# Overlapping two batches of sparse attention beside a shared MLP: adjacency written over the sigmoids, halves across batch ends, tallies on ScalarE, additions on GpSimd

## The reference

```python
# adjacency from ctx (4, 512, 128), mixed into the normalized rows of x, per batch
sim = einsum('bhnd,bhmd->bnm', Q, K) / (sqrt(32) * 4)
threshold = top_k(sim, 153)[0][:, :, -1:]          # the 153rd largest of each row
A = sigmoid(sim) * (sim >= threshold)
A = (A + swapaxes(A, -1, -2)) * 0.5
x = x + tanh(g_xattn[0]) * ((1 - gamma) * layernorm(x) + gamma * A)
# then a mixture of experts with a shared MLP over all rows
shared = silu(xn @ sw1) * (xn @ sw3) @ sw2         # xn = layernorm(x), 704 hidden
```

## Time and profile before

| | us |
|---|---|
| median of three runs | 1753.17 (1752.91 to 1756.59) |
| the profiled execution's own time | 1756.12 |
| its span | 1754.3 |
| stage a, from the span's start to the last `y_in` | 399.9 |
| busy in the span: TensorE, VectorE, ScalarE, GpSimd | 1491.5, 1257.5, 749.7, 458.2 |
| first products of batches 0, 1, 2, 3 start at | 98.15, 181.69, 267.63, 345.61 |

### The profile page before, as it was taken

The page is one execution under the profiler, slowest core; times in us unless marked ns, Lnnn a source line. Parts: engine busy times, 40 slices in busy tenths (PEclk is TensorE's granted clock), DMA queues, the critical chain, the costliest instruction groups (busy, mean ns, idle before and its releaser), DMA issues.

```text
span 1754.3 us, 24078 instructions
## 1 busy us (share of the span) xinstructions
PE 1491.5 (85%) x8146; PEld 713.8 (41%) x8146; DVE 1257.5 (72%) x2199; ACT 749.7 (43%) x1312; POOL 458.2 (26%) x436
## 2 busy tenths in 40 slices
PE   2178687891899999379989999998899999999998
PEld 1145344451555656113223233223444544544544
DVE  6987868736788987699988887864665565555555
ACT  5263535222455554247767776773212212222221
POOL 4212121100566665611000000000232323323222
PEclk7589898996999999679999999999999999999999
DMA  5211212113465554554200202127000000000000
GB/s 172 74 44 45 74 36 84 52 37 111 143 189 183 182 180 145 149 121 97 52 10 17 46 0 49 31 30 139 1 1 0 24 0 0 24 0 0 24 12 12
DMA packets 114805, 113.74 MB, mean 65 GB/s; under 512 B 59416, under 2 KB 87320, under 8 KB 114720
## 3 DMA queue, kind: packets, MB, share of 16 engines
q1 hardware_dynamic: 108752, 93.83, 19.8%
q0 software_dynamic: 5680, 18.62, 3.8%
q10 hardware_dynamic: 288, 0.20, 0.1%
HBM read 59.26 MB, written 31.20 MB: 52 GB/s over the span
## 4 chain that ended last, share of the span: by engine, by line
PE 65%; DVE 20%; issue 5%; ACT 4%; POOL 3%; DMA 2%; SPq 1%; DVEq 0%; ACTq 0%; POOLq 0%
PE PS L1982 18%; PE PS L829 12%; PE PS L2005 9%; PE PS L844 6%; PE PS L1445 5%; DVE WORK L1573 4%; PE PS L1434 4%; PE PS L1425 4%; PE PS L1995 2%; ACT BIG L1343 1%; PE PS L837 1%; PE PS L819 1%; DVE WORK L559 1%; DVE WORK L581 1%; PE PS L417 1%
## 5 line engine op out<-in xcount | busy, mean ns | idle before, releaser
L1982 PE MATMUL PS<-BIG 128*128 128x512 f16 x1536 | 342.6, 384 | 9.2 <-DVE BIG L2060 4.6
L1573 DVE TENSOR_REDUCE WORK<-PS 128x2 f32<-128x1024 f32 x256 | 304.0, 1217 | 46.6 <-PE PS L1425 46.1
L1343 ACT ACTIVATE BIG<-PS 128x512 f32<-128x512 f32 x512 | 278.5, 599 | 102.2 <-PE PS L1434 102.0
L1982 PEld LDWEIGHTS PS<-BIG 128*128 128x128 f16 x1536 | 151.5, 99 | 191.7 <-issue 10.8
L1425 PE MATMUL PS<-BIG 128*128 128x512 f16 x512 | 199.1, 396 | 28.2 <-DVE WORK L1573 19.9
L1434 PE MATMUL PS<-BIG 128*128 128x512 f16 x512 | 195.1, 384 | 7.4 <-ACT BIG L1343 3.0
L829 PE MATMUL PS<-BIG,WORK 128*128 (+1 forms) x1128 | 178.8, 316 | 15.3 <-DVE WORK L864 12.8
L2005 PE MATMUL PS<-BIG 128*128 128x512 f16 x768 | 173.8, 379 | 1.8 <-DVE BIG L2080 1.8
L1918 ACT ACTIVATE WORK<-PS 128x512 f32<-128x512 f32 x64 | 38.2, 597 | 307.5 <-PE PS L1982 307.5
L2060 DVE SCALAR_TENSOR_TENSOR BIG<-PS,WORK 128x512 f32<-128x512 f32 x64 | 44.1, 690 | 141.3 <-ACT WORK L1918 141.2
L829 PEld LDWEIGHTS PS<-BIG,WORK 128*128 128x128 f16 x1128 | 108.9, 98 | 77.0 <-issue 20.1
(11 more groups left out here) (244 smaller groups left out, 2204.4 us busy)
## 6 DMA issues: line engine op xcount, KB each, us to landing
wdq_scratch<-WORK SPq DMA_DIRECT2D x48, 256.0 KB
WORK<-in_L_ffn_w_dram SPq DMA_DIRECT2D x32, 352.0 KB, 3.6
y_scratch<-WORK SPq DMA_DIRECT2D x39, 256.0 KB
BIG<-BIG SPq DMA_DIRECT2D x96, 64.0 KB, 2.3
X<-in_x_dram SPq DMA_DIRECT2D x4, 1024.0 KB, 9.0
WORK<-in_L_ffn_w_dram SPq DMA_DIRECT2D x16, 256.0 KB, 2.8
WORK<-in_L_ffn_gate_w_dram SPq DMA_DIRECT2D x16, 256.0 KB, 3.2
WORK<-in_L_ffn_up_w_dram SPq DMA_DIRECT2D x16, 256.0 KB, 3.2
```

The costliest lines, as they stand in the source:

```text
L1343: nc.scalar.activation(PB[:, tp, 2 * h + j, :], BBANK[j], ACT.Exp, scale=SOFT_SCALE).then_inc(exp_ok, 1)
L1573: v.tensor_reduce(MXU[:, g % 2, c:c + 2], APAIR[h % 2], AX_X, ALU.max, negate=True).then_inc(max_ok, 1)
L1982: ins = nc.tensor.matmul(bank[b], fxT[:, p, a, k * P:(k + 1) * P], w[:, c, l, k, :], start=(i == 0), stop=(i == 3 * KD - 1))
```

## The change

- q and k of batches 1 to 3 lie in used parts of `ctxT`. `adjacency` writes over `sig`, not over `sim`, so the next batch's similarities can be copied into `sim` before this batch is mixed. From batch 1 on, similarities go through bank 0, one at a time.
- The halves of all batches form one sequence: `finish(u - 2)` runs across batch ends, banks alternate (`pair_of`), and the turn of half u-1 comes behind the product of half u, except at i = 6 and 7. The next batch's projection stands at i = 5, its similarities at i = 5, 6, 7, its `search_start` and first try at the end.
- Counts: ScalarE applies Sign to th_try - sim and sums (`counts`), for two of four rows in batch 0 and all rows after it. VectorE's step works with S minus twice the count.
- For batches 1 to 3 ScalarE makes tanh of half the value, GpSimd turns it into the gated half sigmoid (`gains`) and adds the masked rows to X (`own_similarities`); VectorE adds only the turned ones.
- The 14 shared splits stand behind batch 0's tallies, sigmoids and mixes on ScalarE. The stores of normalized rows are issued by ScalarE (`rows_hi`). SP's loads stand in one sequence. Expert splits are spread over the halves as `SPLITS` says. A few semaphores are merged; `MISSED` lies in bank 7.

```diff
 sim = carve(WORK, "sim", 0, [P, R, S])
 ctxT = carve(WORK, "ctxT", 8192, [P, T])
-qT = carve(WORK, "qT", 16384, [P, S])
-kT = carve(WORK, "kT", 18432, [P, S])
+qT = [carve(WORK, "qT", 16384, [P, S])] + [ctxT[:, (b - 1) * S:b * S] for b in range(1, B)]
+kT = [carve(WORK, "kT", 18432, [P, S])] + [ctxT[:, b * S:(b + 1) * S] for b in range(1, B)]
...
+SPLITS = (1, 1, 2, 2, 2, 2, 1, 1)
+def early_chunks(f, i):
...
     for h in range(2):
         load_slot(sp, h, shared_src(h))
-    for t in range(TT):
-        if t == 0:
...
+    for n, e, j in EXPERTS_IN:
+        load_chunk(sp, n, j, expert_src(e))
+    for j in range(NCH):
         load_chunk(sp, 7, j, expert_src(LATE))
...
+    def gains(b):
+        for r in range(R):
+            pool.wait_ge(sig_sb, b * R + (r + 1))
+            nc.gpsimd.tensor_scalar(sig[r], sig[r], GATES[:, 5:6], GATES[:, 5:6], ALU.mult,
+                                    ALU.add).then_inc(own_ok, 1)
+    def own_similarities(b):
+        for r in range(R):
+            xt = X[:, b * R + r, :]
+            pool.wait_ge(xmix, b * R + (r + 1))
+            pool.wait_ge(adj_ok, b * R + (r + 1))
+            nc.gpsimd.tensor_tensor(xt, sig[r], xt, ALU.add).then_inc(own_ok, 1)
     link(nc.gpsimd.memset(ident[:, :], 0.0))
...
+            if i == 2:
+                gains(f + 1)
+            if i == 6:
+                own_similarities(f + 1)
+            for n, e, j in early_chunks(f, i):
+                lo_chunk(pool, n, e, j)
     pool.wait_ge(split_l, 7 * NCH)
     pool.wait_ge(SH.y_mm, TT - R)
     pads(link, [LATE])
...
+    def similar(b, rows):
+        for r in rows:
             act.wait_ge(sim_mm, b * R + (r + 1))
-            nc.scalar.activation(sim[:, r, :], ABANKS[r % 2], ACT.Copy).then_inc(sim_sb, 1)
-    def sigmoids(b, rows):
+            if b:
+                act.wait_ge(adj_ok, (b - 1) * R + (r + 1))
+            nc.scalar.activation(sim[:, r, :], sim_bank(b, r), ACT.Copy).then_inc(sim_sb, 1)
+    def sigmoids(b):
         act.wait_ge(sim_sb, b * R + R)
-        for r in rows:
-            nc.scalar.activation(sig[r], sim[:, r, :], ACT.Sigmoid, scale=SIM_SCALE).then_inc(sig_sb, 1)
+        if b == 0:
+            for r in range(R):
+                nc.scalar.activation(sig[r], sim[:, r, :], ACT.Sigmoid, scale=SIM_SCALE).then_inc(sig_sb, 1)
+        else:
+            act.wait_ge(x1_ok, b * R)
+            for r in range(R):
+                nc.scalar.activation(sig[r], sim[:, r, :], ACT.Tanh, scale=SIM_SCALE / 2).then_inc(sig_sb, 1)
+    def counts(b, n):
+        act.wait_ge(th_ok, b * TRIES + (n + 1))
+        rows = counted_rows(b)
+        for i, r in enumerate(rows):
+            done = counted(b, n) + i
...
+            nc.scalar.activation(signs[b > 0][:, i % 2, :], sim[:, r, :], ACT.Sign, bias=th_try[:, r:r + 1],
+                                 scale=-1.0, accum_out=tally[n % 2][:, r:r + 1]).then_inc(cnt_ok, 1)
...
+    def rows_hi(t):
+        act_hi(act, SH, near(t), t % 2, t)
+        act.wait_ge(SH.x_ok, t + 1)
+        nc.scalar.dma_start(xn_dram[t * P:(t + 1) * P, :], near(t).xn[:, t % 2, :]).then_inc(xn_st[t % 2], 16)
     head(0)
+    similar(0, range(R))
     act.wait_ge(gw_mm, 1)
     nc.scalar.activation(gwT[:, 0, :], bank[7][:, 0:KD * E], ACT.Copy, scale=W_SCALE).then_inc(gw_hi, 1)
-    sigmoids(0, range(R))
-    act.wait_ge(coef_ok, 1)
+    head(1)
+    for n in range(TRIES):
+        counts(0, n)
+    act.wait_ge(cnt_ok, counted(1, 0))
+    sigmoids(0)
+    act.wait_ge(coef_ok, 2)
     mixes(0, range(R))
     for h in range(2):
         split_hi(act, h, E - 2 + h, range(NCH))
...
+    similar(1, range(R))
+    rows_hi(0)
+    counts(1, 0)
+    for f in range(B - 1):
+        a, c, t0 = f + 1, f + 2, f * R
         for i in range(2 * R):
-            t, h, u = t0 + i // 2, i % 2, 2 * t0 + i
-            if i > 0:
+            t, h, u = t0 + i // 2, i % 2, 2 * R * f + i
+            if i in TURN_FIRST:
                 act_thi(act, SH, NEAR, 1 - h, u - 1)
...
+            act_sil(act, SH, NEAR, h, u, pair_of(f, i))
+            if u > 0 and i not in TURN_FIRST:
+                act_thi(act, SH, NEAR, 1 - h, u - 1)
+            if h == 0 and i < 6:
+                rows_hi(t + 1)
+            if i + 1 < TRIES:
+                counts(a, i + 1)
+            if i == 2:
+                sigmoids(a)
+            if i == 3:
+                mixes(a, (0, 1))
+            if i == 4:
+                mixes(a, (2, 3))
+            if i == 5 and c < B:
+                head(c)
+            if i == 6 and c < B:
+                similar(c, (1, 2))
+            if i == 7:
+                if c < B:
+                    similar(c, (3,))
+                rows_hi(t0 + R)
+            for n, e, j in early_chunks(f, i):
                 split_hi(act, n, e, (j,))
...
+            if i == 5 and c < B:
+                similar(c, (0,))
...
+def pair_of(f, i):
+    return 0 if f < B - 1 and i in TURN_FIRST else (i + 1) % 2
+def sim_bank(b, r):
+    return bank[0] if b else ABANKS[r % 2]
...
-    def similarities(b):
+    def similarities(b, rows):
         pe.wait_ge(qk_sb, b * 2 + 2)
...
+        for r in rows:
+            if b and r:
+                pe.wait_ge(sim_sb, b * R + r)
+            if not b and r >= 2:
+                pe.wait_ge(sim_sb, r - 1)
+            nc.tensor.matmul(sim_bank(b, r), qT[b][:, r * P:(r + 1) * P], kT[b], start=True,
+                             stop=True).then_inc(sim_mm, 1)
...
+    similarities(1, range(R))
+    pe.wait_ge(sim_sb, 2 * R)
+    turn_rows(0)
+    pe.wait_ge(split_l, 2 * NCH)
+    for f in range(B):
+        a, c, t0 = f + 1, f + 2, f * R
         for i in range(2 * R):
-            t, h, u = t0 + i // 2, i % 2, 2 * t0 + i
-            if i > 0:
+            t, h, u = t0 + i // 2, i % 2, 2 * R * f + i
+            turn_first = f < B - 1 and i in TURN_FIRST
+            if turn_first:
                 turn_hidden(u - 1)
             pe.wait_ge(SH.tx_lo, t + 1)
-            pe_hg(SH, near(t), t % 2, E - 2 + h, 0 if b < B else h)
+            pe_hg(SH, near(t), t % 2, E - 2 + h, pair_of(f, i))
+            if u > 0 and not turn_first:
+                turn_hidden(u - 1)
             if h == 0:
+                if i == 6 and a < B:
+                    pe.wait_ge(adj_ok, a * R + 1)
                 logits(t)
-                if t + 1 < t0 + R:
+                if i < 6:
                     turn_rows(t + 1)
...
+            if i == 5 and c < B:
+                project(c)
+            if i == 5 and a < B:
+                pe.wait_ge(lg_sb, t + 1)
+                count_missed(a)
+            if i == 6 and a < B:
+                if c < B:
+                    pe.wait_ge(qk_sb, 2 * c + 2)
+                turn(a, (0, 1))
+                if c < B:
+                    similarities(c, (1,))
+            if i == 7 and a < B:
+                if c < B:
+                    similarities(c, (3,))
+                    pe.wait_ge(sim_sb, c * R + R)
+                turn_rows(t + 1)
+            if u > 1:
                 finish(u - 2)
-            if b + 1 < B and i == 7:
-                similarities(b + 1)
+            if i == 5 and c < B:
+                similarities(c, (0,))
+            if i == 6 and a < B:
+                turn(a, (2, 3))
+                if c < B:
+                    similarities(c, (2,))
     finish(2 * TT - 2)
...
+    def search_step(b, n):
+        now, last = tally[n % 2], tally[1 - n % 2]
+        dve.wait_ge(th_ok, b * TRIES + (n + 1))
+        if b == 0:
+            for r in range(R // 2):
+                link(v.tensor_scalar(topw, sim[:, r, :], th_try[:, r:r + 1], None, ALU.is_ge, ALU.add,
+                                     accum_out=rank[:, r:r + 1]))
+            link(v.tensor_scalar(now[:, 0:R // 2], rank[:, 0:R // 2], -2.0, float(S), ALU.mult, ALU.add))
+        dve.wait_ge(cnt_ok, counted(b, n) + len(counted_rows(b)))
         if n:
-            link(v.tensor_tensor(diff, count, last, ALU.subtract))
+            link(v.tensor_tensor(diff, now, last, ALU.subtract))
             link(v.scalar_tensor_tensor(diff, diff, -1.0, diff, ALU.mult, ALU.max))
-            link(v.tensor_scalar(diff, diff, 1.0, None, ALU.max))
+            link(v.tensor_scalar(diff, diff, 2.0, None, ALU.max))
             link(v.reciprocal(diff, diff))
             link(v.scalar_tensor_tensor(step, step, -1.0, step, ALU.mult, ALU.max))
             link(v.tensor_tensor(gain, step, diff, ALU.mult))
-        link(v.tensor_scalar(outside, count, -AIM, None, ALU.add))
+        link(v.tensor_scalar(outside, now, -1.0, S - 2.0 * AIM, ALU.mult, ALU.add))
         link(v.tensor_tensor(step, outside, gain, ALU.mult))
         link(v.tensor_tensor(outside, outside, outside, ALU.mult))
...
+        link(v.scalar_tensor_tensor(step, outside, float(WINDOW ** 2), step, ALU.is_gt, ALU.mult))
+        ins = v.tensor_tensor(th_try, th_try, step, ALU.add)
+        if n + 1 < TRIES:
+            ins.then_inc(th_ok, 1)
+        else:
```

(59 more changed lines are left out.)

208 lines of the change are left out of this document (59 added, 149 removed).

## The result

The changed kernel takes 1759.23 us (median of nine runs, 1756.95 to 1761.72). The kernel before, run beside it, took 1753.17 (nine runs, 1751.57 to 1756.71): ratio 1.0032, 95% interval 1.0022 to 1.0041. The forecast was 1698.0, with 1676 to 1726 as its range: 61 us too low, and the kernel became 0.3% slower instead of faster.

The account below looks back on a forecast made before the run. The prediction took a ring of TensorE's and VectorE's mutual waits as today's bound, VectorE's program as the bound afterwards. Start -9.4, middle stretches -47.2 and last stretch +1.5 sum to -55.1, from 1753.17 to 1698.0 us; range 1676 to 1726.

Parts of the forecast that it names:

- tallies: Middle stretches: VectorE waits for ScalarE's sign counts in tries 0, 1 and 2, taken as 3.6, 1.8 and 2.6 us.
- look-ahead: Middle stretches: TensorE multiplies half u before turning half u-1, which hides a lag of one half.
- smaller edits: Merged semaphores and the count of misses in bank 7: priced at nothing, as adding no instruction to the ring.
- one ring: Middle stretches before the change: product, silu, hid, turn, with search pieces between; TensorE waits 25.7 us for dve_hid.
- Walking VectorE's program: Middle stretches: VectorE's order with its waits sets the period; 54.5 us plus waits gives 67.1.
- the fallback under the check: Slower case: a row outside the window makes check_threshold search four rows, 111 us, giving 1809; chance 0.04.
- The rival on ScalarE's queue: Middle stretches: tallies held in ScalarE's strictly ordered queue, 9 us a stretch, giving 1725; chance 0.14.
- the rival on GpSimd: Middle stretches: each of eight new GpSimd operations costs VectorE its full 1.05 us, 6.4 more a stretch, 1717; chance 0.10.
- a period over 72 us: Middle stretches: the forecast counted itself wrong if the period was under 62 or over 72 us.
- Start: Up to the first product: a shorter search, then splits and similarities; first product at 88.8 against 98.15, -9.4 us.
- Middle stretches: Three stretches of one batch's MLP beside the next's attention: 200.3 us together against 247.5, -47.2 us.
- Last stretch: MLP alone: inherits two second products and loses most of 3.5 us of idle TensorE, +1.5 us.

Follow-up runs that it names:

- Runs 1 and 2: Changed kernel with y_in alone moved: first to the head of the even half (y_head), 1731.36 us; then among the pieces of search (y_mid), 1711.54 us.
- y_mid: Changed kernel with y_in alone taken out of half and placed among the pieces of search; 1711.54 us, ratio 0.9773 to the kernel before.
- mid_pad: y_mid plus 32 empty instructions in ScalarE's program ahead of its part of layer 1's attention; 1709.52 us, ratio 0.9767 to the kernel before.
- Run 6: y_mid with the kernel before's order, turn of half u-1 before product of half u, for batches 0 to 2; 1717.91 us, ratio 0.9812.
- y_head: Changed kernel with y_in alone moved back to the head of the even half; 1731.36 us, ratio 0.9890 to the kernel before.

## Why the prediction was wrong

**The step that failed is one that the sum does not have.** The forecast went through "tallies", "look-ahead", "mix", and priced "smaller edits" at nothing, since "they add no instruction to the ring". The new place of `y_in`, from the head of `half` to its back, stands in the diff; it adds no instruction, so by that rule it was priced at nothing, and it closes a second ring: product, silu, hid, `y_in`, second product, next product. TensorE waited 40.7 us for it in the three stretches, and the last one grew by 16.8 instead of 1.5. The first part had drawn one ring, through hid and the turn, and read TensorE's wait for it as the thing to win. The question that would have found it is the one to ask of every bank: who frees it, what stands ahead of that in its queue, and who is behind the one that waits? "Walking VectorE's program" looked only for VectorE's own waits. Runs 1 and 2 price the omission: 28 us for the place within `half`, 48 for a place that suits the new order.

**No rival had it.** The only slower case was the fallback under the check, which did not run. The rival on ScalarE's queue asked for more waiting for tallies than forecast, and there was less; the rival on GpSimd asked for 6.4 us more a stretch, and in the second stretch VectorE's busy time came out 2.1 us above the forecast. The mechanism that decided was neither. One of the forecast's own signs of being wrong, a period over 72 us, was met in all three stretches (74.34, 84.86, 82.55).

Step by step, against the changed kernel and against `y_mid`, which is the kernel that the forecast had in mind:

- *Start*, forecast -9.4, first product at 88.8: measured 87.38. Right; the window's start was forecast for 42.9 and came at 42.16. The splits run from 44.65 (forecast 47.2) to 75.9, 31.3 us (forecast 31.0). The similarities did wait behind them.
- *Tally*, 0.85 taken: the pitch is 0.71 us.

```profile
38.18 0.72 ACT L387 ACTIVATE WORK<-WORK 128x512 f16<-128x512 f32 x1 [2.46 <-DVE WORK L675]
38.81 0.19 ACT L387 ACTIVATION_READ_ACCUMULATOR WORK<-WORK 128x1 f32 x1
38.90 0.71 ACT L387 ACTIVATE WORK<-WORK 128x512 f16<-128x512 f32 x1
```

  The waits for tallies were forecast at 3.6 + 1.8 + 2.6 = 8.0 us a stretch; 17.5 us in three were measured, 5.8 each.
- *Middle stretches*, forecast 67.1, 67.1, 66.1, together 200.3: in `y_mid` 72.57, 67.46, 64.89, together 204.9. With the ring away the walk through VectorE's program was right to 5 us; in `mid_pad`, with the same stage a, to 8 (208.4). Some of that is luck, since errors of opposite sign met: the tallies cost 2 us a stretch less than forecast, and in the second stretch of `y_mid` 4.8 us went into two waits that the walk did not have, 3.2 for a turned half and 1.6 in front of `y_in`. In the kernel after: 241.8.
- *Look-ahead.* The forecast priced no term with it, but argued from it that TensorE's waits vanish. Run 6 puts it at 6.4 us for all three.
- *Clock*, "I take full clock": 0.86 to 0.88 in the kernel after, 0.89 to 0.95 in `y_mid`. It is higher where TensorE pauses less.
- *GpSimd*, 2.0 us a stretch: VectorE's busy time without that term was forecast at 50.4 in the second stretch and is 54.54 after, 52.69 in `y_mid`: 4.1 and 2.3 more, if all of it is put down to GpSimd. Gains took 0.77 each, additions 1.28 each in the second stretch (1.05 taken).
- *Tables.* Two tables in and two out a stretch were there before. After, the first silu loads one (1.28 us, at 93.86), and no other load follows in the three stretches, though Silu, Tanh and Sign alternate.
The Trainium skill, ScalarE: Activation LUTs, section "Table sets", names tanh beside exp and sigmoid and not beside silu, from which the forecast read two loads a batch; the trace has none, and it decides.
- *Last stretch*, +1.5, to 55.8: 71.1 after; 56.8 in `y_mid` and in `y_head`.
- *What follows keeps its length*: not quite. +3.6 us after, +5.9 in `y_mid`; the stop on ScalarE is 4.3 and 4.4 us long.

`y_mid` stands 13.5 us above the forecast: 4.2 from stage a (349.05 against 399.93 - 55.1 = 344.8), 5.9 behind it, and 3.4 from the difference of median to span, which was -1.1 in the profiled kernel before and is +2.2 here.

## What to carry to other kernels

When the order of a pipeline is rewritten, list every buffer with who frees it, and ask what stands ahead of the freeing instruction in its queue; a consumer moved by one place costs nothing on its own engine and can hold the engine across. A wait that one engine has for another is worth removing only as far as the other's program gets shorter: the order of turn and product, with 19.4 us of such waits, was worth 6.4. And look at the stretch where the change should do nothing: its 17 us pointed at the cause before any experiment did.
